# A transformer decoder layer on one core: softmax denominators summed by ScalarE over the max pass, and stacks loaded by pairs of heads

## The reference

```python
q = heads(hidden_states @ Wq)
k = heads(hidden_states @ Wk)
v = heads(hidden_states @ Wv)
scores = jnp.einsum('bhqd,bhkd->bhqk', q, k) / jnp.sqrt(jnp.float32(D))
attn = jax.nn.softmax(scores, axis=-1)
std = jnp.einsum('bhqk,bhkd->bhqd', attn, v)
std = std.transpose(0, 2, 1, 3).reshape(b, s, hid) @ Wo
...
return (1.0 - blend) * std + blend * dgsa
```

## Time and profile before

| | us |
|---|---|
| median of 3 runs | 1584.42 (1580.32 to 1585.39) |
| profiled execution, its own time | 1582.52 |
| its span in the trace | 1580.8 |
| PE busy | 1226.0 (78%) |
| DVE busy | 1246.4 (79%) |
| ACT busy | 759.4 (48%) |
| POOL busy | 213.3 (13%) |

### The profile page before, as it was taken

The page is one execution under the profiler, slowest core; times in us unless marked ns, Lnnn a source line. Parts: engine busy times, 40 slices in busy tenths (PEclk is TensorE's granted clock), DMA queues, the critical chain, the costliest instruction groups (busy, mean ns, idle before and its releaser), DMA issues.

```text
span 1580.8 us, 14027 instructions
## 1 busy us (share of the span) xinstructions
PE 1226.0 (78%) x4570; PEld 570.7 (36%) x4570; DVE 1246.4 (79%) x1485; ACT 759.4 (48%) x1110; POOL 213.3 (13%) x247
## 2 busy tenths in 40 slices
PE   4664746778688897778888886878888887788796
PEld 3332212223244442323344532323344532333453
DVE  5867978777989996885889995785889995877534
ACT  6775425435366632545466642545466633534232
POOL 1000221000111132100111132000111132001000
PEclk8756878779789898879889997789889998779798
DMA  6843794555439868451249776451248777462131
GB/s 196 272 161 109 168 222 118 115 118 111 101 82 234 211 171 215 94 140 34 62 118 238 184 194 178 94 144 30 62 120 237 183 182 182 92 150 41 36 105 66
DMA packets 112151, 220.15 MB, mean 139 GB/s; under 512 B 14048, under 2 KB 24800, under 8 KB 112080
## 3 DMA queue, kind: packets, MB, share of 16 engines
q1 hardware_dynamic: 92704, 151.24, 32.9%
q0 software_dynamic: 18432, 67.12, 21.9%
q10 hardware_dynamic: 944, 0.92, 0.2%
HBM read 122.37 MB, written 29.62 MB: 96 GB/s over the span
## 4 chain that ended last, share of the span: by engine, by line
DVE 39%; PE 28%; issue 10%; DMA 6%; ACT 3%; SPq 1%; POOL 1%; DVEq 0%; ACTq 0%; POOLq 0%
DVE ST L874 14%; DVE ST L866 6%; PE ps L1463 5%; PE ps L1264 5%; DVE MX L930 5%; PE ps L1281 4%; DMA KS<-qk_parts 3%; PE ps L1416 2%; DVE RD L1077 2%; DVE ST L877 2%; DVE QAK L1092 2%; PE ps L1373 2%; PE ps L1432 2%; PE ps L1345 2%; DVE BST L910 1%
## 5 line engine op out<-in xcount | busy, mean ns | idle before, releaser
L874 DVE TENSOR_TENSOR_SCAN ST<-dA,ST 128x1024 f32<-128x1024 f32 x128 | 311.8, 2436 | 8.8 <-ACT dA L577 6.0
L930 DVE TENSOR_REDUCE MX<-ps 128x1 f32<-128x512 f32 x256 | 165.3, 686 | 117.5 <-PE ps L1264 117.4
L1463 PE MATMUL ps<-V,GU 128*128 128x512 f16 x1024 | 243.3, 394 | 5.6 <-DVE V L1059 5.6
L471 POOL DMA_DIRECT2D YA<-ST x128 | 111.0, 867 | 1012.2 <-DVE ST L877 953.9
L1264 PE MATMUL ps<-KS,QS 96*128 96x512 f32 x256 | 134.1, 599 | 116.0 <-DVE MX L930 53.0
L577 ACT ACTIVATE dA<-DL,Aneg 128x511 f32<-128x511 f32 x256 | 168.9, 713 | 82.9 <-DVE ST L874 82.6
L709 ACT ACTIVATE PT<-ps 128x1024 f32<-128x1024 f32 x128 | 126.4, 1021 | 124.4 <-PE ps L1373 123.7
L1432 PE MATMUL ps<-WP,QS 128*128 128x512 f32 x512 | 145.8, 429 | 28.3 <-DMA WP<-proj_tiles 20.6
L877 DVE TENSOR_TENSOR ST<-ST,BC 128x1024 f32<-128x1024 f32 x128 | 159.4, 1246 | 4.4
L866 DVE TENSOR_TENSOR ST<-DU,BC 128x1024 f32<-128x1024 f32 x128 | 156.8, 1225 | 6.7 <-DMA BC<-bc_rows 6.5
L1463 PEld LDWEIGHTS ps<-V,GU 128*128 128x128 bf16 x1024 | 98.2, 101 | 139.2 <-issue 32.1
(11 more groups left out here) (230 smaller groups left out, 1606.9 us busy)
## 6 DMA issues: line engine op xcount, KB each, us to landing
YA<-ST POOLq DMA_DIRECT2D x128, 512.0 KB, 7.3
BC<-bc_rows SPq DMA_DIRECT2D x64, 512.0 KB, 6.3
qk_parts<-PT SPq DMA_DIRECT2D x64, 256.0 KB, 6.3
GU<-gu_tiles SPq DMA_DIRECT2D x64, 256.0 KB, 9.1
WP<-proj_tiles SPq DMA_DIRECT2D x64, 256.0 KB, 6.7
QS<-qk_parts SPq DMA_DIRECT2D x48, 256.0 KB, 5.3
KS<-qk_parts SPq DMA_DIRECT2D x48, 256.0 KB, 5.9
ST<-in_L_ffn_w_gate_up_dram SPq DMA_DIRECT2D x16, 256.0 KB, 3.5
```

What stands on the lines that cost most here:

```text
L874: nc.vector.tensor_tensor_scan(flat, dA[:, a, :, :].rearrange("p e s -> p (e s)"), flat, 0.0, ALU.mult, ALU.add).then_inc(s_scan, 1)
L930: nc.vector.tensor_reduce(MX[:, j % 2, qt, h:h + 1], ps[:, n % 2, :], AX_X, ALU.max).then_inc(s_mx, 1)
L1463: last = mm(ps[:, f % F_RING, :], GU[:, t % GU_RING, k, m * P:(m + 1) * P], XHL[:, z, k, :], start=(k == 0 and z == 0), stop=(k == KT - 1 ...
```

## The change

Four things change together.

1. **Denominators.** ScalarE takes, for every tile of the max pass, exp of the bank minus the row's maximum, in place, with the sum over the 512 keys as a second output (`max_exps`). VectorE's maximum is made negated, since it serves as the bias. The products of PT with ones and their use of bank 7 are gone. Scale and sign move: q is multiplied by the scale when it is read, the splat readings undo it, and the bias row is a copy.
2. **Inverse.** VectorE takes the reciprocal of the 16 columns of sums (`invert`), ScalarE widens them to 32 columns a head (`widen_inverse`), TensorE turns them with the identity into bank 7 (`spread_inverse`), ScalarE reads that with the blend's factor into RD (`inverse_rows`), and VectorE normalises with one product in place of three passes.
3. **Banks.** A bank of the max pass is free when its exp is done (`s_me`), no longer when its maximum is. From group 1 on, bank 7 joins banks 0 and 1 from tile 6 on.
4. **Stacks.** `load_stack` issues 12 DMAs of two heads each in place of 6 of four heads, first pair first, with a semaphore for each pair; the max pass waits for its pair alone.

The core of the diff:

```diff
+        MAX_BANKS = ((0, 1) * 8, (0, 1, 0, 1, 0, 1, 7, 0, 1, 7, 0, 1, 7, 0, 1, 7))
+
+        def max_bank(j, m):
+
+            return MAX_BANKS[j > 0][m]
+
+        def max_steps(j, kt):
+
+            tiles = X_CHUNK[j][kt:kt + 2] if j + 1 < NG else (0, 0)
+            steps = (0, 0, 4, 4) if j > 0 and kt == 0 else (0, 2, 4, 6)
+            return [min(tiles[0] + n, tiles[1]) for n in steps] + [tiles[1]]
+
+        def fill_steps(r):
+
+            lo, hi = X_FIRST[r - 3 * KT:r - 3 * KT + 2] if r >= 3 * KT else (0, 0)
+            return [min(lo + n, hi) for n in ((0, 0, 2) if r == 3 * KT + 1 else (0, 2, 4))] + [hi]
...
-                for r, (zq, zk) in enumerate(((0, 0), (0, 1), (1, 0))):
-                    for z, dst, part in ((0, QS[i], zq), (1, KS[i], zk)):
-                        src = qk_parts[b, z, part, P * j:P * j + P, :].rearrange("(h p) s -> p h s", p=D)
-                        sp.dma_start(dst[D * r:D * r + D, :, :].bitcast(F32), src).then_inc(s_stack[i], 16)
+                for pair in range(HG // 2):
+                    first_row = P * j + 2 * D * pair
+                    for r, (zq, zk) in enumerate(((0, 0), (0, 1), (1, 0))):
+                        for z, dst, part in ((0, QS[i], zq), (1, KS[i], zk)):
+                            src = qk_parts[b, z, part, first_row:first_row + 2 * D, :].rearrange("(h p) s -> p h s", p=D)
+                            sp.dma_start(dst[D * r:D * r + D, 2 * pair:2 * pair + 2, :].bitcast(F32), src).then_inc(s_stack[i][pair], 16)
...
-            def inverse_start(b, j):
-
-                act.wait_ge(s_pv, KT * NG * b + KT * (j + 1))
-                nc.scalar.activation(RD[:, :], ps[:, 7, :], ACT.Ln).then_inc(s_lnd, 1)
-                act.wait_ge(s_lnd, NG * b + j + 1)
-                nc.scalar.activation(RD[:, :], RD[:, :], ACT.Exp, scale=-1.0).then_inc(s_rd, 1)
+            def widen_inverse(b, j):
+
+                act.wait_ge(s_rdn, NG * b + j + 1)
+                if j < 2:
+                    act.wait_ge(s_aff, 2 * b + 2)
+                else:
+                    act.wait_ge(s_rd, NG * b + j - 1)
+                nc.scalar.activation(X1[:, j % 2, :].rearrange("p (q h d) -> p q h d", q=KT, h=HG),
+                                     RDEN[:, :, :].unsqueeze(3).broadcast_to((P, KT, HG, D)), ACT.Copy).then_inc(s_rdx, 1)
+
+            def inverse_rows(b, j):
+
+                act.wait_ge(s_rd, NG * b + j + 1)
+                if j > 0:
+                    act.wait_ge(s_nrm, NG * b + j)
+                else:
+                    since(act, s_rms, b)
+                nc.scalar.mul(RD[:, :], ps[:, 7, :], par[:, ONEMB:ONEMB + 1]).then_inc(s_rdc, 1)
+
+            def max_exps(b, j, lo, hi):
+
+                if lo == 0 and hi > 0:
+                    since(act, s_rdn, NG * b + j - 1)
+                for m in range(lo, hi):
+                    h, qt = m // KT, m % KT
+                    act.wait_ge(s_mx, 16 * NG * b + 16 * j + m + 1)
+                    bank = ps[:, max_bank(j, m), :]
+                    nc.scalar.activation(bank, bank, ACT.Exp, bias=MX[:, j % 2, qt, h:h + 1],
+                                         accum_out=DEN[:, j % 2, qt, h:h + 1]).then_inc(s_me, 1)
...
+                    by = SCALE if UNITS[u][1] == 0 else 1.0
+                    cuts = fill_steps(2 * KT + u)
+                    max_exps(b, 0, cuts[0], cuts[1])
                     act.wait_ge(s_fill, 4 * KT * b + 2 * KT + u + 1)
                     if u >= 2:
                         act.wait_ge(s_gsa, NG * b + u // 2)
                         act.wait_ge(s_lo, 2 * NG * b + u - 1)
-                    nc.scalar.copy(PT[:, 0, u % 2, :], bank)
-                    nc.scalar.square(PT[:, 0, 2 + u % 2, :], bank).then_inc(s_q32, 1)
+                    nc.scalar.mul(PT[:, 0, u % 2, :], bank, by)
+                    nc.scalar.activation(PT[:, 0, 2 + u % 2, :], bank, ACT.Square, scale=by ** 0.5).then_inc(s_q32, 1)
                     if u >= 2:
                         act.wait_ge(s_part[u % 2], 32 * KT * b + 32 * (u // 2))
-                    nc.scalar.copy(QKP[:, u % 2, :], bank).then_inc(s_hi, 1)
+                    nc.scalar.mul(QKP[:, u % 2, :], bank, by).then_inc(s_hi, 1)
+                    max_exps(b, 0, cuts[1], cuts[3])
                     for n, a in fill_halves(2 * KT + u, first):
                         exp_dA(b, n, a)
                 bias_row(b, 0)
                 for z in range(2):
-
+                    by = 1.0 / SCALE if z == 0 else 1.0
                     act.wait_ge(s_gsa, NG * (b + 1))
                     since(act, s_out, 16 * KT * b)
                     nc.scalar.activation(X1[:, 2 * z, :], ps[:, 2 + 2 * z, :], ACT.Relu,
-                                         bias=par[:, POSSQ:POSSQ + 1]).then_inc(s_dist, 1)
+                                         bias=par[:, POSSQ:POSSQ + 1], scale=by).then_inc(s_dist, 1)
                     nc.scalar.activation(X1[:, 2 * z + 1, :], ps[:, 3 + 2 * z, :], ACT.Square,
-                                         bias=par[:, NPD:NPD + 1]).then_inc(s_pj2, 1)
+                                         bias=par[:, NPD:NPD + 1], scale=by).then_inc(s_pj2, 1)
+                max_exps(b, 1, 0, X_AHEAD)
...
+                        cuts = max_steps(j, kt)
...
-                                                 ACT.Exp, scale=SCALE).then_inc(s_exp, 1)
+                                                 ACT.Exp).then_inc(s_exp, 1)
+                            max_exps(b, j + 1, cuts[p], cuts[p + 1])
+                        max_exps(b, j + 1, cuts[2], cuts[4])
+                        if kt == 2:
+                            widen_inverse(b, j)
...
-                    nc.vector.tensor_reduce(MX[:, j % 2, qt, h:h + 1], ps[:, n % 2, :], AX_X, ALU.max).then_inc(s_mx, 1)
+                    nc.vector.tensor_reduce(MX[:, j % 2, qt, h:h + 1], ps[:, max_bank(j, i), :], AX_X, ALU.max,
+                                            negate=True).then_inc(s_mx, 1)
+
+            def invert(b, j):
+
+                dve.wait_ge(s_me, 16 * NG * b + 16 * (j + 1))
+                since(dve, s_rdx, NG * b + j)
+                nc.vector.reciprocal(RDEN[:, :, :], DEN[:, j % 2, :, :]).then_inc(s_rdn, 1)
 
             def normalise(b, j):
 
-                dr, vr = X1[:, 0, :], X1[:, 1, :]
-                dve.wait_ge(s_rd, NG * b + j + 1)
-                nc.vector.tensor_tensor(dr, ps[:, 7, :], RD[:, :], ALU.mult)
-                nc.vector.scalar_tensor_tensor(out=vr, in0=ps[:, 6, :], scalar=par[:, NONEMB:NONEMB + 1],
-                                               in1=RD[:, :], op0=ALU.mult, op1=ALU.mult).then_inc(s_nrm, 1)
-                dve.wait_ge(s_nrm, NG * b + j + 1)
-                nc.vector.scalar_tensor_tensor(out=XA[:, j, :], in0=dr, scalar=2.0, in1=vr,
-                                               op0=ALU.subtract, op1=ALU.mult).then_inc(s_wrd, 1)
+                dve.wait_ge(s_pv, KT * NG * b + KT * (j + 1))
+                dve.wait_ge(s_rdc, NG * b + j + 1)
+                nc.vector.tensor_tensor(XA[:, j, :], ps[:, 6, :], RD[:, :], ALU.mult).then_inc(s_nrm, 1)
...
+                        if c == 1:
+                            invert(b, j)
...
-                if lo == 0 and hi > 0:
-                    pe.wait_ge(s_stack[i], 96 * (2 * b + j // 2 + 1))
                 if lo == 0 and hi > 0 and j == 0:
                     pe.wait_ge(s_hi, 2 * NG * b + 4)
                 for m in range(lo, hi):
                     n = 16 * j + m
                     h, qt = m // KT, m % KT
-                    if n >= 2:
-                        pe.wait_ge(s_mx, 16 * NG * b + n - 1)
+                    if m % (2 * KT) == 0:
+                        pe.wait_ge(s_stack[i][h // 2], 96 * (2 * b + j // 2 + 1))
+                    bank = max_bank(j, m)
+                    same = [q for q in range(n) if max_bank(q // 16, q % 16) == bank]
+                    if same:
+                        pe.wait_ge(s_me, 16 * NG * b + same[-1] + 1)
+                    if bank == 7 and 7 not in MAX_BANKS[j > 0][:m]:
+                        pe.wait_ge(s_hi, 2 * NG * (b + 1))
+                        since(pe, s_rdc, NG * b + j - 1)
                     if j > 0 and m == 0:
                         since(pe, s_br, NG * b + j)
                     if j == 2 and m == 1:
                         pe.wait_ge(s_ka, b + 1)
-                    mm(ps[:, n % 2, :], QS[i][0:3 * D, h, qt * P:(qt + 1) * P], KS[i][0:3 * D, h, :],
+                    mm(ps[:, bank, :], QS[i][0:3 * D, h, qt * P:(qt + 1) * P], KS[i][0:3 * D, h, :],
                        start=True, stop=True).then_inc(s_xs, 1)
 
             def transpose_max(b, j):
                 pe.wait_ge(s_mx, 16 * NG * b + 16 * (j + 1))
+                pe.wait_ge(s_me, 16 * NG * b + 16 * j + max(m for m in range(16) if max_bank(j, m) == 0) + 1)
                 for qt in range(KT):
                     last = nc.tensor.transpose(ps[0:HG, 0, qt * P:(qt + 1) * P], MX[:, j % 2, qt, :], ident[:, :])
```

(40 more changed lines are left out.)

28 lines of the change are left out of this document (15 added, 13 removed).

## The result

| | before | after |
|---|---|---|
| median, us | 1584.24 (1580.32 to 1585.39) | 1663.46 (1661.55 to 1665.67) |
| ratio | | 1.0505, 95% interval 1.0483 to 1.0528 |
| profiled execution, its own time / span | 1582.52 / 1580.8 | 1663.91 / 1662.2 |

The change makes the kernel 79 us slower. The forecast was slower by 44 us, 1628 us with a range to 1660: the sign is right, the size is too small, and the time lies 3.5 us above the range.

What follows compares the result with a forecast made beforehand. The prediction saw VectorE, TensorE and ScalarE waiting for each other, with ScalarE becoming the bound in group 0. Batches 1 to 3 add 40 us and batch 0 adds 4: 1584.4 + 44 = 1628 us, range 1596 to 1660.

Steps and rivals of the forecast that it cites:

- The likeliest case: Whole kernel: slower as forecast, exp between 0.61 and 0.95 us, +27 to +70, 1611 to 1654 us; chance 0.65.
- Rival 1: Whole kernel: ScalarE's idle time swallows the exps, so faster, 1524 us or about 1550; chance 0.12.
- (a) to (c): Fill, batch 1: max tiles or the projection wait for late exps, +3.35, +2.95 and +2.0 us; transposes +8.3.
- (b): Fill: tiles 8 and 9 wait for exps of 6 and 7, which stand behind unit 6's readings, +2.95 us.
- Price of the exp: Each max tile: ScalarE's exp with its sum takes 0.75 us, between 0.61 and 0.95; 48 us a batch.
- (d) and (e): Group 0: ScalarE's work delays the next scores by 16.6 us; group 1: stack wait goes, first max tile shifted +13.4.
- without a hole: Group 0: ScalarE runs its readings, exps, inverse and bias row back to back, 28.45 us, to 668.0.
- Batches 1 to 3 are alike: Batches 1 to 3: batch 1's +13.4 us applies to each, +40 in all.
- Group 2 and group 3: Per batch: group 2, with normalisation not between the tiles, +3.5 us; group 3, without max pass, -4.7 us.
- Batch 0: First batch: VectorE's scan halves cover most of the fill's delays, and ScalarE's sum passes VectorE's by little: +4 us.
- Stack pairs: Stack loads: earlier start removes group 1's 4.16 us wait; longer SyncE queue costs nothing, at the worst +2.6 a batch.
- rival 4: Group 0: TensorE's clock falls too, its work becomes 26 us, 3 to 8 us more a batch, 1640 to 1660; chance 0.06.

Runs made afterwards that it cites:

- e4: Changed kernel without exps over the banks, each bank free at its maximum, one exp a group standing in for the sums: 1532.6 us, ratio 0.970.
- g1: Changed kernel with full-length exps at the same places but reading and writing SBUF, banks free at the maximum: 1583.2 us, ratio 0.9997.
- e5: Changed kernel with the fill's exps of sums written ahead of unit casts and of the readings of units 6 and 7: 1637.3 us, ratio 1.0348.
- e1: Kernel before with only the stack loads cut into pairs of heads, a semaphore for each pair: 1552.8 us, ratio 0.9824.
- e2: Changed kernel with whole stacks again, six DMAs in place of pairs: 1691.5 us, ratio 1.0715.
- h1: Changed kernel with 27 unused identity products a batch in group 0, written to bank 7, group 1's max tiles on two banks: 1678.1 us, ratio 1.0611.
- h2: Changed kernel with fill exps earlier, splat exps and affinities later, plus unused identity products in group 0, group 1's max tiles on two banks: 1641.0 us, ratio 1.037.
- e3: Changed kernel with exps of sums over 8 of the 512 columns, all waits unchanged: 1611.4 us, ratio 1.0194.

## Why the prediction was too small

- **Direction and reason: right.** The likeliest case was TensorE held at a bank behind exps that stand behind other work. e4, g1 and e5 show it: no exps -131, bank released at the maximum -80, order of the fill -26. Rival 1 (idle time swallows the exps) is ruled out: ScalarE is idle 44% of the span and 131 us are paid all the same.
- **Fill, (a) to (c): right.** +8.3 forecast for batches 1 to 3, +7.7, +6.3 and +9.0 measured. The projection behind tile 3 comes 2.4 us later against the start of the fill (I had 3.35). Unit 7's first reading comes 6.1 us later (6.3). The terms of (b) add up to 2.80, not to the 2.95 that stand there, which changes nothing.
- **Price of the exp: too high, and it didn't save the sum.** I took 0.75 us. In a row the exps start 0.66 us apart (631.56 to 632.22): the reading of the sum is an instruction of its own of 0.2 us, but it lies beside the end of one exp and the start of the next. The prediction's estimate from the Trainium skill's "ScalarE: Activation LUTs" (What ACT_TABLE_LOAD costs) was 0.71 us for an exp with a pointer as bias; the rows say 0.665 for this one over a bank and 0.717 for the same over SBUF in g1.
- **Group 0 and the start of group 1, (d) and (e): the step that failed in batches 1 to 3.** I added up ScalarE's instructions to 28.45 us "without a hole" and made the scores of group 1 end at 670.5, 16.6 us late. They end at 696.32, which is 98.7 us after the fill's start in place of 77.1: 21.7 late. The instructions of the sum ran from 661.36 to 693.68, 32.3 us. The sum was not too small: ScalarE is busy 27.0 us of these, 1.5 less than I had. What failed is "without a hole": 5.3 us of waits, 4.6 of them for maxima. That is 3.9 of the missing 5.1 us; most of the rest is that the list starts 1.1 us later than I had it, behind splat products at the lower clock. When TensorE waits for ScalarE and ScalarE for VectorE and VectorE for TensorE, no engine's busy time sets the stage. Groups 0 and 1 together were to cost 5.1 + 1.2 = 6.3 us a batch. They cost 14.1, 11.6 and 13.0. "Batches 1 to 3 are alike" was wrong too: group 0 before took 18.7, 23.3 and 20.1 us, so it lost 14.8, 10.1 and 13.4. g1, where the ring is cut, has a stage bound by ScalarE as forecast (25.9 us). The smaller terms: the spreading products take 1.4 us a group (22.8 in all) where I had 0.6.
- **Group 2 and group 3: right.** +3.5 forecast, +3.7, +3.3 and +3.5 measured; -4.7 forecast, -4.6, -4.5 and -2.7 measured.
- **Batch 0: the largest single miss.** I gave it +4 because scan halves fill VectorE there; it has +20.8: fill +9.0, group 0 +14.2, group 1 -1.5, group 2 +2.0, group 3 -2.9. The cover doesn't exist: what waits is TensorE. The windows of batch 0, fill and group 0, after:

```profile
182.22:260.51 78.29, 42.27 (x104) 15.41 (x104) 58.01 (x44) 33.77 (x73) 19.00 (x18) 0.79 0.79 195
260.51:299.87 39.36, 24.28 (x76) 10.05 (x73) 24.39 (x31) 26.24 (x55) 4.16 (x4) 0.69 0.21 46
```

 VectorE, busy 22.8 of 25.2 us in group 0 before (251.42 to 276.62), is busy 24.4 of 39.4 now. A busy VectorE doesn't hide a ring that runs through it, since it is one of its links. How much of the wait is that of its scans no run shows. By the stages of e4, exps and wait cost batch 0 32 us and batch 1 34.5.
- **Stack pairs: sized at one wait of 4.16 us a batch, worth 7.** e1 and e2 give 28 us. The stack waits fell by 32 us in e1, more than the one I had put down, and in the changed kernel the wait for the bias row goes too (e2). The price that I gave SyncE's longer queue ("at the worst +2.6 a batch") doesn't show.
- **The clock: the fall is right, its chance too low, its price open.** Group 0 of batch 1 fell from 1.00 to 0.65 and TensorE's work there took 24.8 us (26 in rival 4). I gave that 0.06 and the time 1640 to 1660. The Trainium skill's "TensorE: Matmul & The Clock Gate" (A second HAM failure mode: psum-queue depth-cycling) had spoken for it: short idles between groups of products make the clock go back and forth. On the fall of the clock the trace of batch 1 agrees with the page. Rival 4's 3 to 8 us a batch are neither shown nor ruled out: h1 and h2 show no gain, the stages at two clocks show 1.9 to 4.7 us in other kernels. The time fell outside that rival as well. I had also taken 1.00 for the clock of group 0 in all the batches 1 to 3, and batch 2 stood at 0.71 before the change.

In numbers, by the spans: the miss is 81 - 44 = 37 us. Batch 0 is 17 of it; groups 0 and 1 of batches 1 to 3 are 20 (39 in place of 19); group 3 adds 2 and the fill takes 2 back. The range ended at 1660 for the same reason: it had bounds for the price of an exp and for a falling clock, and none for holes in a ring or for a batch 0 like the others. The sign was right by reasoning; that the miss of the range is as small as 3.5 us is partly luck, as stack pairs that I had put at little gave 28 us back.

## What to carry to other kernels

When a buffer's release is moved from one engine to a second that works in order, look first at what stands ahead of the releasing instruction, not at its length: here 80 of 131 us hung on the release, and a third buffer gave nothing in the order of the change. Where three engines wait for each other in a ring, don't price a stage by the busiest engine's sum, and don't count another engine's work as cover. Look at a stage in every repetition before calling them alike. Measure the parts of a bundled change alone: half of this one (stacks by pairs, and one pass of normalisation) is worth 42 us here and was buried under the other.

## What the runs showed of the hardware

- The sum of an activation is read by an instruction of its own, 206 ns. An exp of 512 columns over a bank takes 665 ns, one of 8 columns 244 ns (e3).

```profile
L691 ACT ACTIVATION_READ_ACCUMULATOR ps<-ps,MX 128x1 f32 x256 | 52.8, 206 | 0.0
```

```profile
L691 ACT ACTIVATE ps<-ps,MX 128x8 f32<-128x8 f32 x256 | 62.2, 244 | 182.1 <-DVE MX L985 181.9
```

- In batch 1, from the issue of a bias row of 8 KB to the scores that need it, 7.2 us passed behind six DMAs of 256 KB (e2), 4.1 behind six of 128 KB (changed kernel).
- The granted clock of group 0 in batch 1 stood at 1.00 before; it was 0.65 with waits of 0.2 to 2.6 us between TensorE's products. In batch 2 the same stage stood at 0.71 already before the change, and took 4.7 us more than in batch 1.
- Products that nobody uses, put in beside those waits, raised it to 0.77, and the time with it (h1).
